# Mixing head: single columns of the up bias strewn between key and query products, six fillers for ten, and the four messages in the layers' slots

## The reference

```python
def _linear_attn(x, Wq, Wk, Wv, Wo, bo):
    ...
    q = jax.nn.softmax(split(x @ Wq) * scale, axis=-1)
    k = jax.nn.softmax(split(x @ Wk) * scale, axis=-2)
    v = split(x @ Wv)
    context = jnp.einsum('bhnd,bhne->bhde', k, v)
    out = jnp.einsum('bhnd,bhde->bhne', q, context)
    ...
for i in range(DEPTH):
    h = _layernorm(x, ln1_g[i], ln1_b[i])
    x = x + _linear_attn(h, Wq[i], Wk[i], Wv[i], Wo[i], bo[i])
    h = _layernorm(x, ln2_g[i], ln2_b[i])
    x = x + (jax.nn.gelu(h @ W1[i] + b1[i], approximate=False) @ W2[i] + b2[i])

# graph part, one message for each of 50000 edges
messages = h_fwd[src] * direction[:, 0:1] + h_rev[src] * direction[:, 1:2]
```

## Time and profile before

| | |
|---|---|
| median of 3 runs | 2792.88 us (2789.84 to 2804.66) |
| the profiled execution's own time | 2785.83 us |
| its span | 2784.1 us |
| TensorE matmuls busy | 2408.1 us (86%) |
| TensorE weight loads busy | 2252.8 us (81%) |
| VectorE busy | 1835.6 us (66%) |
| ScalarE busy | 1397.9 us (50%) |
| GpSimd busy | 1249.9 us (45%) |

### The profile page before, as it was taken

How to read it: one execution, slowest core, us unless ns; L and a number is a source line. 1 busy time by engine, 2 the same in 40 slices (tenths; PEclk the granted TensorE clock), 3 DMA queues, 4 the chain that set the end, 5 groups by cost and what they waited for, 6 DMA issues and landing times. The chain is left out here.

```text
span 2784.1 us, 47683 instructions
## 1 busy us (share of the span) xinstructions
PE 2408.1 (86%) x16282; PEld 2252.8 (81%) x16282; DVE 1835.6 (66%) x4645; ACT 1397.9 (50%) x3051; POOL 1249.9 (45%) x1406
## 2 busy tenths in 40 slices
PE   7888999899989998996997799656776888888898
PEld 6778998899889988996777799546776688888798
DVE  5665877677767776656776465466756666666665
ACT  4334655465646554554643344332233555555687
POOL 1323553344424542555874322336665566665100
PEclk9989999999999999998995799868888899999899
DMA  5211112111211121125333555346653366566011
GB/s 111 72 35 39 39 46 69 36 41 42 73 31 42 43 57 34 47 57 114 92 84 101 154 159 154 99 144 172 176 168 114 88 182 188 170 184 187 18 40 31
DMA packets 150452, 259.91 MB, mean 93 GB/s; under 512 B 35793, under 2 KB 96044, under 8 KB 150086
## 3 DMA queue, kind: packets, MB, share of 16 engines
q0 software_dynamic: 49632, 145.61, 19.4%
q1 hardware_dynamic: 100582, 111.25, 13.5%
HBM read 219.96 MB, written 36.82 MB: 92 GB/s over the span
## 5 line engine op out<-in xcount | busy, mean ns | idle before, releaser
L988 POOL DMA_INDIRECT gat<-table,srcT x400 | 414.1, 1035 | 364.4 <-DVE m L2892 235.5
L1146 POOL DMA_INDIRECT x_rows<-table,srcT x392 | 403.0, 1028 | 251.3 <-issue 113.9
L646 PE MATMUL pa<-w,act 128*125 128x256 f32 x2400 | 360.3, 288 | 15.4 <-DVE act L2651 13.8
L646 PE MATMUL pb<-hT,w 128*128 128x378 f32 (+1 forms) x1920 | 337.9, 312 | 9.3 <-ACT gf L2040 8.3
L646 PEld LDWEIGHTS pa<-w,act 128*125 128x125 f32 x2400 | 315.4, 188 | 20.3 <-DVE act L2651 18.4
L646 PEld LDWEIGHTS pb<-hT,w 128*128 128x128 f32 x1920 | 287.2, 190 | 13.7 <-ACT gf L2040 8.5
L2340 ACT ACTIVATE gf<-pb,bne 128x378 f32<-128x378 f32 (+1 forms) x320 | 194.4, 607 | 190.4 <-PE pb L646 136.8
L2040 ACT ACTIVATE gf<-pb,b1s 128x378 f32<-128x378 f32 (+1 forms) x320 | 166.0, 519 | 116.7 <-PE pb L646 90.0
L2651 DVE TENSOR_TENSOR act<-gf,act 128x378 fp32r<-128x378 f32 (+1 forms) x320 | 153.9, 483 | 100.4 <-ACT act L2043 72.8
L646 PE MATMUL pb<-xT,fw 128*128 128x378 f32 (+1 forms) x960 | 164.1, 322 | 5.1 <-ACT gf L2340 4.6
L3654 DVE TENSOR_TENSOR act<-gf,act 128x378 fp32r<-128x378 f32 (+1 forms) x180 | 87.2, 488 | 118.6 <-ACT act L2344 75.6
(11 more groups left out here) (534 smaller groups left out, 5804.2 us busy)
## 6 DMA issues: line engine op xcount, KB each, us to landing
e<-in_L_ffn_W_dram SPq DMA_DIRECT2D x40, 512.0 KB, 6.0
spill<-m SPq DMA_DIRECT2D x80, 170.0 KB
msg<-spill SPq DMA_DIRECT2D x40, 340.0 KB, 2.9
yslots<-yo SPq DMA_DIRECT2D x64, 128.0 KB, 2.2
fraw<-in_L_ffn_W_dram SPq DMA_DIRECT2D x32, 256.0 KB
w1r<-in_L_mix_W_dram SPq DMA_DIRECT2D x7, 1024.0 KB, 4.8
gat<-table,srcT POOLq DMA_INDIRECT x400
x_rows<-table,srcT POOLq DMA_INDIRECT x392
```

Source lines behind the costliest of these rows:

```text
L646: mm = nc.tensor.matmul(ps, lhs(l), rhs(r), start=first and n == 0, stop=last and n == 2)
L988: pool.indirect_dma_start(out=gat[:, i % 2, c, :], out_offset=None, in_=table0, in_offset=bass.IndirectOffsetOnAxis(ap=srcT[:, i * GC + c: ...
L1146: pool.indirect_dma_start(out=x_rows[:, n % UB, c, :].bitcast(F32), out_offset=None, in_=table1, in_offset=bass.IndirectOffsetOnAxis(ap=sr ...
```

## The change

The 16 single columns of a round (up bias of one layer) leave the round's end. They stand between the key and query products of the first two pairs: one behind each half product of pair 0, two behind each half product of pair 1. They go to bank 0 of `u_ring`. The filler ahead of `sum_context` has six matmuls for ten, and takes bank 1, in which `spread_max` has just put its result. VectorE adds b1 earlier, behind `n_lower` of the third pair. The four messages leave the head; each slot with g = 0 makes four for three, the fourth in step 12. SyncE loads the three W1 one after the other without message stores between.

```diff
-MSG_HEAD = 4
+MSG_HEAD = 0
-MSG_SLOT = (3, 4, 4, 4, 4)
+MSG_SLOT = (4, 4, 4, 4, 4)
...
-        for i in range(MSG_HEAD):
-            if i + 1 < NL:
-                sp.wait_ge(s["b1_ps"], i + 1)
-                bias_load(NL - 2 - i)
-            store_message(i)
+        for l in reversed(range(NL - 1)):
+            sp.wait_ge(s["b1_ps"], NL - 1 - l)
+            bias_load(l)
...
-            if g:
-                fetch_next(g - 1)
...
-        def row_product(p, lhs, place, rhs, to):
+        def row_product(p, lhs, place, rhs, to, beside=()):
             first, n = PAIRS[p]
+            parts = iter(beside)
             for i in range(n):
                 for h in range(H):
                     last = hi_lo_products(to[0:TP, i * D:(i + 1) * D], lambda k: lhs[k][:, h, place[first + i], 0:TP],
                                           lambda k: rhs(k, h), h == 0, h == H - 1)
+                    for f in next(parts, ()):
+                        up_bias(*f)
...
+        def up_bias(l, f, h):
+            mm = nc.tensor.matmul(u_banks[0][:, f:f + 1], w1r[:, h, f * P:(f + 1) * P], lnb[:, l, 1, h:h + 1],
+                                  start=h == 0, stop=h == H - 1)
+            if (f, h) == (FT - 1, H - 1):
+                mm.then_inc(s["b1_ps"], 1)
...
+            biases = [[(NL - 1 - g, f, h)] for f in range(FT) for h in range(H)] if g < NL else []
+            if g < NL:
+                pe.wait_ge(s["sm_ld"], 16 * 5 * NL)
+                pe.wait_ge(s["w1b"], 16 * (g + 1))
+                u_ring[0].take(pe)
+                u_ring[0].used = (s["b1_ready"], g + 1)
+            k_product(0, g, 0, d_ring[0], biases[0:4])
+            q_product(0, g, 0, head_q[0], biases[4:8])
+            k_product(0, g, 1, d_ring[1], [a + b for a, b in zip(biases[8:12:2], biases[9:12:2])])
+            q_product(0, g, 1, head_q[1], [a + b for a, b in zip(biases[12:16:2], biases[13:16:2])])
...
-                keep_warm(10)
+                keep_warm(6, 1)
...
-            if g < NL:
-                up_bias(NL - 1 - g)
...
-                if n == 12 and MSG_SLOT[g] > 3:
+                if n == 12:
                     message(first + 3)
...
             n_lower(0, g, 2)
+            if g < NL:
+                up_bias(NL - 1 - g)
...
             if g:
-                message(g - 1)
```

More of the change, by code:

```diff
@@ L1330, in row_product, with k_product, q_product @@
                                           lambda k: rhs(k, h), h == 0, h == H - 1)
+                    for f in next(parts, ()):
+                        up_bias(*f)
             return last
-        def k_product(l, g, p, ring):
+        def k_product(l, g, p, ring, beside=()):
             J = 3 * group(l, g) + p
             pe.wait_ge(s["n_lo"], J + 1)
-            row_product(p, nT, RING, lambda k, h: wqk[k][:, h, D:2 * D], ring.take(pe)).then_inc(s["kp_ps"], 1)
+            row_product(p, nT, RING, lambda k, h: wqk[k][:, h, D:2 * D], ring.take(pe), beside).then_inc(s["kp_ps"], 1)
             ring.used = (s["k_ev"], J + 1)
-        def q_product(l, g, p, ring):
+        def q_product(l, g, p, ring, beside=()):
             J = 3 * group(l, g) + p
             pe.wait_ge(s["n_lo"], J + 1)
-            row_product(p, nT, RING, lambda k, h: wqk[k][:, h, 0:D], ring.take(pe)).then_inc(s["qp_ps"], 1)
+            row_product(p, nT, RING, lambda k, h: wqk[k][:, h, 0:D], ring.take(pe), beside).then_inc(s["qp_ps"], 1)
             ring.used = (s["q_ev"], J + 1)
@@ L1518, in _ @@
             turn_n(0, g, 1)
-            for p in range(2):
-                k_product(0, g, p, d_ring[p])
-                q_product(0, g, p, head_q[p])
+            biases = [[(NL - 1 - g, f, h)] for f in range(FT) for h in range(H)] if g < NL else []
[8 more added lines that the diff above has]
+            q_product(0, g, 1, head_q[1], [a + b for a, b in zip(biases[12:16:2], biases[13:16:2])])
             if g:
@@ L2871, in up_bias @@
             dve.wait_ge(s["b1_ps"], NL - l)
-            nc.vector.tensor_tensor(b1s[:, l, :], bias_bank()[:, 0:FT], b1c[:, l, :], ALU.add).then_inc(s["b1_ready"], 1)
+            nc.vector.tensor_tensor(b1s[:, l, :], u_banks[0][:, 0:FT], b1c[:, l, :], ALU.add).then_inc(s["b1_ready"], 1)
         def down_bias(l):
```

## The result

| | before | changed |
|---|---|---|
| median of 6 runs each, same chip | 2791.36 us (2774.19 to 2804.66) | 2817.08 us (2805.84 to 2824.58) |
| ratio | | 1.0095, 95% interval 1.0067 to 1.0123 |
| profiled execution, its span | 2785.83, 2784.1 us | 2824.58, 2822.8 us |

A forecast was written before the change was run, and what follows sets the result against it. TensorE was taken to bound the slots and nearly all of a head round, with ScalarE's work hidden under the column block. Head -1.4 and messages +3.4 gave +2.0 us: 2795 against 2792.88, range 2785 to 2807.

The forecast's parts named there:

- The terms for rounds 0 and 3: Head: the gain there is used up by columns running slow, about 1 us and 0.6 us more; each about 0.
- the term for round 2: Head, between rounds 2 and 3: -3.4 from VectorE's earlier query sum, +2.56 columns, +0.15 filler, giving -0.7 us.
- the columns starve the clock: Rival: strewn products of pairs 0 and 1 stay at the lower clock, +5 us in each of four rounds, 2815; chance 0.08.
- The price of a strewn column: Head products of pairs 0 and 1: 0.14 us per column, 0.36 a pair, 2.56 a round against the block's 3.49.
- hidden columns: Rival: strewn columns cost nothing, their weight loads hidden under long streams; another -10 us, 2785; chance 0.10.
- The end of a round: Last query product to next key product: without the block ScalarE sets the time, 5.9 us for 9.53, saving 3.6.
- Fillers: Ahead of `sum_context`: six fillers run beside the exponential after VectorE's subtraction, TensorE 0.15 us late in four rounds.
- Messages: Nothing back in the head; TensorE waits in slots (1, 0), (2, 0), (3, 0) of 0.9, 0.9, 1.6 us more, together +3.4.
- The lower clock in slot (3, 0): Rival: TensorE's wait there grows from 1.03 to 2.6 us and brings the clock down, +1.7, 2797; chance 0.25.
- The clock stays up in every round: Rival: slow products of head rounds 3 and 4 are saved too, about 1 us each, 2793; chance 0.15.

The follow-up runs named there:

- the second profile: The changed kernel itself, unaltered, run again on a faster chip: 2677.62 us, 1.0084 of the kernel before; its head ends at 225.49.
- the two pairs of profiles: Changed kernel against itself with its messages back in the head (2818.86 us); kernel before against itself with four messages in slots g = 0 (2797.09 us).
- messages alone: Kernel before with the four messages moved to the slots with g = 0, block of columns and ten fillers kept: 2797.09 us, 1.0006 of before.
- strewn, warm: Changed kernel with more fillers ahead of the first products and under waits for VectorE (9, 9, 17, 17 ahead of `turn_max`): 2789.90 us, 0.9977 of before.
- dense strewn: Changed kernel with each strewn matmul streaming 128 columns of ones instead of one column (up bias wrong): 2664.27 us, 1.0028 of before.

## Why the prediction was wrong, step by step

**The step that failed** is the clock in the sum. The terms for rounds 0 and 3 knew that the products start at half clock there, and added 1 us and 0.6 us for the columns at that rate, as if the clock came back as early as in the kernel before; the term for round 2 had no slow stretch at all. By the sum round 0 was worth 0 us, round 3 about 0 and round 2 -0.7. Measured are +6.7, +8.7 and +8.9 (the stretches of these rounds in the table). In before, dense products bring the clock back: in round 0 twelve of them take 2.69 us, and in round 3 the first twelve take 2.65, and full speed follows. With single columns between them it stayed at half for 20.4 us in round 2 and 24.0 in round 3, although TensorE worked without a gap over the products; with 128 columns for one it was back in 3.4.

The prediction had this mechanism among its rivals, *the columns starve the clock*, at a chance of 0.08. The sentence against it read a stretch between 222.20 and 230.50 with idle time, transposes and fillers at clock 1.00. That stretch shows work that *held* a full clock. It says nothing of work that has to *bring back* a clock that is down, and the rows of the slow starts were at hand. That the rival's time, 2815, is so near 2817.08 is in part luck: it priced four rounds at +5 each, and three were lost, at +6.7 to +8.9, one of which kept its clock in the second profile. Round 1 is the case that I had in mind, held at 1.00 over 7.8 us.

The Trainium skill (TensorE: Matmul & The Clock Gate, Part 1) says that the gate follows how busy the engine has been recently. The busy share of this case's profile doesn't tell the two cases apart: TensorE was busy 7.80 of 7.80 us at clock 1.00 and 14.43 of 14.43 at 0.50.

**The price of a strewn column.** Forecast 0.14 us, a pair 0.36. Measured at full clock 0.22: a group of three products and a column takes 0.57 us, three products alone 0.36 (the 4.48 us less one column, over 36 products, are 0.12 each). A pair takes 0.43: a group with two columns is 0.79 us (113.40 - 112.61 by the starts of its products), less 0.36. All sixteen take 3.3 to 3.5 us, as the block does: nothing is hidden. The 0.03 at the start of the block was read as a load under the stream before; what it is instead no run shows. With 3.5 us for 2.56 the sum gives 0.0 for round 1 and not -0.9, and 0.0 (0.05 less) is what was measured. The rival *hidden columns* is refuted by the same numbers.

**What else the sum had.** *The end of a round* was right: `hk` is followed at once by the transposes (0.25 us), and `turn_max` starts 4.59 us behind the last query product in round 2 for a forecast 4.7, and 6.48 in round 3 for 6.5. What I priced at nothing is the idle time in this, 0.76 us and 2.65, for the clock: round 3 was at half clock behind it, and whether the 0.76 us helped to bring down round 2 is open. *Fillers*: `sum_context` follows `spread_max` by 3.70 us (119.50 - 115.80) for 3.47, +0.2 for a forecast 0.15. *Messages*: the waits are 0.89, 0.92 and 2.60 us for forecast 0.9, 0.9 and 2.6. But the sum had them give nothing back in the head, and they gave 5.3 and 5.6 us by the marks. In the totals this can't be seen: from the head's end to the end of the layers the two pairs of profiles are 7.9 and 4.4 us longer with the messages in the slots, and what that has beyond 3.4 no run shows. *The lower clock in slot (3, 0)* was a rival within the forecast, +1.7: behind the wait six products take 1.64 us at clock 0.50 for 0.97, and the second `mix_up` starts 3.94 us after them for 2.56 (1153.85 - 1149.91, 1126.99 - 1124.43), so 1.4 us later. In *messages alone* the same wait did not bring it down (0.98). *The clock stays up in every round* was put at 2793, no change; the nearest to it is *strewn, warm*, at 0.9977 of before.

**What isn't settled.** The span of the changed kernel's profile is 38.7 us over before's. 22 of them are the head, and at the end of the layers the offset is 22.4 us; the rest arises in the last graph stage, where both kernels have the same code. Both profiled executions lie off their medians, by 7.5 us upward and 5.5 downward, which is just the 13.0 us between 38.7 and the 25.7 of the medians; no run shows what makes this spread. In the second profile of the changed kernel the head ends 13.0 us behind that of before, and the medians there differ by 22.2; before has no profile on that chip, so the two can't be set side by side. And no run separates the idle time from the columns in what brings the clock down in round 2; the block shows only that 32 thin instructions behind dense work can do it without any idle time.

## What to carry to other kernels

Thin matmuls (of a single column) weren't free filling between dense ones: each took 0.22 us, as in a block, and where the clock was down it stayed down while they were interleaved. Ask of a change of TensorE's order not only whether the clock holds, but where it is already down and what brings it back there, and keep that stretch dense. Where TensorE waits for another engine ahead of such a stretch, fillers fit under the wait: here they took 25.8 us off the changed kernel's head. That brought the total back to before and not clearly below it.

## What the runs showed that I had not expected

- The same work ran at either clock: interleaved single columns at 1.00 for 7.8 us in round 1, and at 0.50 for 14.4 us in round 3.
- A matmul of 128x128 weights in f32 costs 0.22 us between others whether it streams 1 column or 128, and with the wide one the clock comes back: 1.0028 for *dense strewn* against 1.0084 for the changed kernel.
- Three products and their column take 1.06 us at half clock for 0.57 at full, less than twice.
- Messages that were thought to lie in VectorE's idle time cost the head 5 us: without them TensorE waits less ahead of `turn_max`.
